# Moving half of four causal masks from VectorE to ScalarE and GpSimd, with two score banks instead of three

## The reference, cut to what matters

```
x = x + attention(layernorm(x))      # 16 heads of 16, chunks of 128 tokens
    q, k = elu(x Wq) + 1, elu(x Wk) + 1 ;  v = x Wv
    per chunk: scores = q k^T, kept where key <= query, else 0
               num = scores v + q S ;  S = S + k^T v
               out = num / (q . (running sum of k))
x = x + 0.5 * (silu(h w1 + b1) w2 + b2)   # h = layernorm(x) * gamma + beta
    w = (int - 128) * scale per group of 128 rows
```

## Time and profile before

| | |
|---|---|
| median of 3 runs | 1573.81 us (1571.97 to 1579.19) |
| the profiled execution's own time | 1571.97 us |
| its span | 1570.2 us |
| busy: PE, PEld, DVE, ACT, POOL | 97%, 84%, 83%, 72%, 43% |
| granted PE clock, mean | 0.993 |

### The profile page before, as it was taken

How to read it: one execution, slowest core, us unless ns; L and a number is a source line. 1 busy time by engine, 2 the same in 40 slices (tenths; PEclk the granted TensorE clock), 3 DMA queues, 4 the chain that set the end, 5 groups by cost and what they waited for, 6 DMA issues and landing times.

```text
span 1570.2 us, 40671 instructions
## 1 busy us (share of the span) xinstructions
PE 1529.8 (97%) x14820; PEld 1314.5 (84%) x14820; DVE 1307.1 (83%) x2587; ACT 1128.3 (72%) x1917; POOL 670.7 (43%) x466
## 2 busy tenths in 40 slices
PE   5799999999999999999999999999999999999997
PEld 4588888888888888888888888888888888888887
DVE  6888888888888888888888888888888888888875
ACT  4487677787777787777786776786776786777863
POOL 3244334544344444344444344443445443435443
PEclk9899999999999999999999999999999999999999
DMA  6945775445775556764556764447664556755450
GB/s 190 206 114 129 174 174 130 137 119 135 174 171 122 126 131 145 174 170 125 119 127 153 174 149 138 123 118 166 174 151 130 121 120 174 174 130 137 116 114 28
DMA packets 153945, 222.96 MB, mean 142 GB/s; under 512 B 20033, under 2 KB 71489, under 8 KB 153921
## 3 DMA queue, kind: packets, MB, share of 16 engines
q1 hardware_dynamic: 152560, 222.63, 58.8%
q10 hardware_dynamic: 1360, 0.01, 0.1%
HBM read 138.69 MB, written 83.89 MB: 142 GB/s over the span
## 4 chain that ended last, share of the span: by engine, by line
PE 84%; DVE 11%; issue 2%; DMA 1%; ACT 1%; SPq 1%; DVEq 0%; POOL 0%; ACTq 0%
PE ring L326 35%; PE num L494 7%; PE ring L388 6%; PE ring L389 6%; PE sc L326 5%; DVE probs L615 5%; PE sc L452 5%; PE num L461 3%; PE num L326 3%; PE state_acc L326 3%; DVE xt_lo L645 2%; PE ring L526 2%; PE state_acc L475 2%; DVE silu_f L701 2%; PE state_acc L452 1%
## 5 line engine op out<-in xcount | busy, mean ns | idle before, releaser
L1009 POOL TENSOR_TENSOR s_lo<-silu_f,s_hi 128x512 fp32r<-128x512 f32 x256 | 342.8, 1345 | 524.1 <-ACT s_hi L881 524.0
L615 DVE TENSOR_TENSOR probs<-sc,causal 128x512 f32<-128x512 f32 x416 | 270.6, 683 | 21.7 <-PE sc L452 18.6
L326 PE MATMUL ring<-w_hi,s_hi 128*128 128x256 f32 x992 | 281.5, 284 | 1.0 <-issue 1.0
L326 PE MATMUL ring<-w_lo,s_hi 128*128 128x256 f32 x992 | 278.3, 281 | 0.0
L326 PE MATMUL ring<-w_hi,s_lo 128*128 128x256 f32 x992 | 278.2, 280 | 0.0
L701 DVE SCALAR_TENSOR_TENSOR silu_f<-ring,scale,silu_f 128x512 f32<-128x512 f32 x222 | 166.3, 749 | 72.5 <-ACT silu_f L870 71.2
L326 PEld LDWEIGHTS ring<-w_hi,s_hi 128*128 128x128 f32 x992 | 186.8, 188 | 14.8 <-issue 13.5
L1025 POOL TENSOR_TENSOR qk<-qk,phi_q 128x512 f32<-128x512 f32 x64 | 83.1, 1298 | 264.6 <-DVE qk L668 264.6
L870 ACT ACTIVATE silu_f<-ring,bias,scale 128x512 f32<-128x512 f32 x217 | 168.4, 776 | 34.9 <-PE ring L389 33.9
L388 PE MATMUL ring<-gt_hi,w_q 128*128 128x512 f32 x441 | 192.5, 437 | 0.0
L326 PEld LDWEIGHTS ring<-w_lo,s_hi 128*128 128x128 f32 x992 | 187.0, 189 | 1.3
(11 more groups left out here) (189 smaller groups left out, 3859.2 us busy)
## 6 DMA issues: line engine op xcount, KB each, us to landing
k_stack<-k_rows SPq DMA_DIRECT2D x192, 256.0 KB, 4.0
q_stack<-q_rows SPq DMA_DIRECT2D x384, 128.0 KB, 6.1
k_rows<-silu_f SPq DMA_DIRECT2D x128, 256.0 KB, 3.7
q_rows<-probs SPq DMA_DIRECT2D x128, 256.0 KB, 4.0
x_in<-in_x SPq DMA_DIRECT2D x32, 512.0 KB, 8.3
xb<-in_x SPq DMA_DIRECT2D x32, 512.0 KB, 8.2
out<-clip SPq DMA_DIRECT2D x64, 256.0 KB, 7.8
silu_f<-in_q SPq DMA_DIRECT2D x2, 512.0 KB, 9.8
```

The lines of the kernel that those rows point to most:

```text
L326: last = e.matmul(target, a, b, start=(n == 0), stop=(n == 3 * len(pairs) - 1))
L615: masked[r].done(e.tensor_tensor(half_probs(u, r), score_bank(u, r)[:, :].rearrange("p (h q) -> p h q", h=HV), causal[:, None, :].to_broad ...
L1009: sl.done(e.tensor_tensor(s_lo[:, j, :], silu_f[:, j % SLOTS, :], s_hi[:, j, :].bitcast(F32), ALU.subtract))
```

## The change

It does six things.

1. The third bank for scores is given up: half r is always in `sc[r]`. A half now waits for the half r of the tile before it to be read.
2. For u = 2, 3, 4 and 5 the half r = 1 is no longer masked by DVE. ACT copies it out of PSUM into `probs` (`copy_scores`), and POOL multiplies it by `causal` in place.
3. DVE does `ffn_sum(2)` before `mask(1)`, and the second `snapshots` after `mask(3)` instead of `mask(2)`.
4. In step 0 `weights_2` moves on DVE from behind `mask(7)` to a place ahead of `mask(6)`, and `weights_2_lo` from the end of the step to the place that `weights_2` had. ACT's part moves with it. The products are made in place, in `res` and `x1`, and DVE no longer waits for `x_hat` to be free. POOL's wait for `bias_o` ahead of step 0 is dropped.
5. In step 31 PE does `fc2(1)` before the output product `wo`, not behind it, and DVE does `final(0)` before the adds of `wo`.
6. In step 32 DVE makes `res` ahead of `gt_lo`, and `ffn_scaled(1)` ahead of `ffn_sum(0)`.

```diff
-        SCORES = {(0, 0): 0, (0, 1): 1, (1, 0): 0, (1, 1): 1, (2, 0): 0, (2, 1): 1, (3, 0): 0, (3, 1): 2,
...
+        POOL_MASKS = (2, 3, 4, 5)
+        VE_MASKS = [range(U), [u for u in range(U) if u not in POOL_MASKS]]
+        masked = [ev(f"masked{r}", len(VE_MASKS[r])) for r in range(2)]
+        copied, po_masked = ev("copied", len(POOL_MASKS)), ev("po_masked", len(POOL_MASKS))
...
# pe_iteration, scores(u)
-                    before = score_before(u, r)
-                    if before:
-                        w.need(masked[before[1]], 0, before[0])
-                    elif score_bank(u, r) is state_acc:
-                        w.need(snap, 0)
+                    if r and u - 1 in POOL_MASKS:
+                        w.need(copied, 0, POOL_MASKS.index(u - 1))
+                    elif u:
+                        need_masked(w, u - 1, r)
...
-            if N:
-                fc2(1)
+            fc2(1)
             if A:
                 w.need(at_l)
                 for n in range(2):
                     pe_tokens(e, w, "o", (gt_hi, gt_lo), f"wo{n}", present, wo_pe)
-            if not N:
-                fc2(1)
...
# ve_iteration
-                for r in range(2):
+                for r in range(1 if u in POOL_MASKS else 2):
                     mask_half(e, w, u, r)
...
+            ffn_sum(2)
             if A:
                 mask(1)
-            ffn_sum(2)
-            if A:
                 snapshots(0)
...
                     if u == 5:
                         attention(0)
+                        if preparation[2]:
+                            preparation[2]()
...
-            if preparation[2]:
-                preparation[2]()
+            if preparation[1]:
+                preparation[1]()
             next_features(0)
...
# ac_iteration
+            def copy_scores(u):
+                if A and u in POOL_MASKS:
+                    w.need(sc_pe, 0, u)
+                    w.need(av_pe, 0, u - 2)
+                    copied.done(e.activation(half_probs(u, 1), sc[1][:, :].rearrange("p (h q) -> p h q", h=HV), ACT.Copy))
+
             for j in range(3, FT - 1):
                 ffn_scaled(j)
                 if j in (3, 5):
                     reciprocals_out((j - 3) // 2)
+                copy_scores(j - 1)
                 ffn_silu(j - 1)
...
# po_iteration
             for j in range(2, FT):
+                if A and j in POOL_MASKS:
+                    w.need(copied, 0, POOL_MASKS.index(j))
+                    po_masked.done(e.tensor_tensor(half_probs(j, 1), half_probs(j, 1),
+                                                   causal[:, None, :].to_broadcast([P, HV, P]), ALU.mult))
...
-            ve_iteration(e, -1, False, False, True, True, (projections, None, weights_1))
+            ve_iteration(e, -1, False, False, True, True, (projections, weights_1, None))
```

52 lines of the change are left out of this document (18 added, 34 removed).

## The result

The changed kernel takes 1585.32 us (median of 7 runs, 1584.51 to 1587.36), the kernel before, run beside it, 1571.97 us (median of 7, 1569.71 to 1579.19). The ratio is 1.0084, 95% interval 1.0065 to 1.0103: slower by 13 us. Its profiled execution took 1583.21 us with a span of 1581.5, against 1571.97 and 1570.2 before, so the traces have 11.3 us between them to explain.

What follows compares the result with a forecast made beforehand. The prediction took PE's long row of matmuls, with one hole per step, to bound the kernel. 1571.97 (span 1570.2) + 11.7 + 3.1 + 2.7 = 1589.5 us, taken as 1590; the range holding 8 in 10 was 1577 to 1604.

Steps and rivals of the forecast that it cites:

- The loop: In the 30 full steps, the projection comes 0.39 us later per step, 11.7 us in all.
- The step that failed: On ACT, four copies exceed its slack, so ffn_scaled(7) starts 0.6 us late, at about 762.9 instead of 762.26.
- the forecast's own rule: On DVE, ffn_sum(7) follows the start of ffn_scaled(7) after 0.78 us plus 0.12 for handing over, at 763.8.
- The rest of the chain: Late ffn_sum(7) delays tile 6's masks, second half of scores(7), values(6) to 766.20 and projection to 767.0, where it was 766.64.
- PE's hole: On PE ahead of the projection, a wait for DVE's xt_lo in which PE stands for 0.37 us each step.
- The hole's owner: Ahead of the projection, ACT's xt_hi also bounds xt_lo; only about 0.1 us of the 0.37 us is DVE's.
- Step 0: Early weights_2 waits for the scales, delaying the projection by 5.4 us; 2.3 won back at the end, sum +3.1 us.
- Steps 31 and 32: POOL's later queue and fc2(1) ahead of wo delay x_hat, gt_lo and ffn_sum(0); sum +2.7 us.
- Relief: In the loop, DVE's saved 2.4 us mask tile 6 sooner and close the hole; 1575 or 1561 us, chance 0.07.
- Only the ends: Copies fit into ACT's waits, the loop stays at 47.4 us and the ends cost 5.8; 1578 us, chance 0.13.
- POOL sets the pace: In the loop PE waits for POOL's products at four tiles, 1.2 us a step more; 1626 us, chance 0.12.

Runs made afterwards that it cites:

- experiment 11: The changed kernel with the weights late again in step 0 and steps 31 and 32 in the old order; 1579.57 us, ratio 1.0050.
- experiment 1: The changed kernel with the third score bank and its table put back; 1581.01 us, ratio 1.0058.
- experiment 5: The kernel before with only the second half of tile 5 copied by ACT and masked by POOL, three banks; 1578.83 us, ratio 1.0052.
- Experiment 6: The kernel before with PE's x_transposes moved ahead of values(5), no mask taken off DVE; 1572.87 us, ratio 1.0003.
- experiment 2: The kernel before with two score banks and nothing else changed; 1575.52 us, ratio 1.0023.
- experiment 3: The changed kernel with tile 5's second half masked by DVE again; 1592.62 us, ratio 1.0137.
- experiment 7: The kernel before with early x_transposes and tile 6's second half copied by ACT behind ffn_scaled(7) and masked by POOL; 1565.31 us, ratio 0.9959.
- Experiment 4: The kernel before with four more ACT copies per step into a spare tile nobody reads, DVE keeping all masks; 1580.18 us, ratio 1.0047.

## Why the prediction was right, and where it was off

The forecast, slower and about 1590 us, came true with 1585.3. It was made of three terms. The loop's was too large, three times by the means and twice like with like, and the two of the ends came out 1.8 us too small.

**The loop: +11.7 us forecast, +3.8 measured.** The step that failed is ACT's: `ffn_scaled(7)` was to start 0.64 us late. In the step shown, which has the long form as that of before, it starts 43.45 us behind the last projection instead of 42.99, so 0.46 late. The sum behind it was 2.0 + 0.4 - 1.8 = 0.6 between `ffn_scaled(3)` and `ffn_scaled(7)`; it measured 0.48. The four copies took 0.47 to 0.49 us each from start to start, as put in. But of the 0.4 us for waits on scores only some 0.1 came, ahead of the first copy, that of tile 2; the other three follow their neighbours at once.

From there the forecast's own rule holds: 762.26 + 0.46 + 0.76 + 0.12 = 763.60 for `ffn_sum(7)`, and it comes 44.33 us behind the last projection, which is 763.60 on the times of before. DVE had reached it at 763.45 before, so it is late by 0.15, where I had 0.35. The rest of the chain was right in its mechanism and its size: from 763.60 it gives 766.0 for `values(6)` and 766.8 for the projection, and measured are 766.03 and 766.85. `values(6)` is 0.59 late (forecast 0.76), PE's hole takes 0.38 of it, and the projection is 0.21 late, 0.20 over all long steps, where I had 0.39. A small excess that must first fill a hole is a difference of differences, and 0.18 us too much on ACT became 0.19 in every step. Thirty steps at 0.20 are 6.0 us. That the traces show 3.8 is the mix of forms, which my forecast knew nothing of, and which the change of the loop doesn't fix: with the same loop experiment 11 has 25 long steps. My own range for the step (0.15 to 0.7) holds the 0.20 and not the 0.13.

The forecast's two parts of the loss are both there, in other shares. 0.14 us come through ACT: `ffn_sum(7)` comes 44.32 us behind the last projection instead of 44.18, and it does so with three banks (experiment 1) and with the single copy ahead of `ffn_silu(5)` (experiment 5) as well. 0.06 come through the two banks: the projection follows `ffn_sum(7)` after 3.25 us instead of 3.19. I had blamed the sum of all four copies. How many there are matters little, since the copies of tiles 2 to 4 fall mostly into ACT's waits: between 90 and 1500 us ACT waited 33 us for the blocks of `fc1` before and waits 1 us now. What counts is the one next to `ffn_scaled(7)`.

**The hole's owner.** I wrote that it was ACT's `xt_hi` as much as DVE's `xt_lo`. Experiment 6 shows that `xt_hi` alone is not worth anything: 47.34 against 47.36. In the six traces with three banks and tile 6 left to DVE the projection comes 3.18 to 3.20 us behind `ffn_sum(7)`, which is that sum, two masks and two `xt_lo` on DVE; in the five of the changed loop it is 3.25, where PE's own row behind the second mask sets it; with two banks and tile 5 left to DVE (experiments 2 and 3) it is 3.48; only where a mask behind `ffn_sum(7)` was taken away and the transposes came early too is it 2.81. That the mask of tile 6 would do without the early transposes was not tried.

**Step 0: +3.1 forecast, +4.2 measured.** DVE waits for the scales (4.14 us; 3.8 forecast), and the projection of step 0 comes at 62.56 (60.7 forecast): the products start 1.0 us later than I had (56.76 against 55.8), and PE's row ahead of the projection, at the lower clock, lets it start only 1.05 us behind the end of `xt_lo`. (The term itself adds up to 5.4 + 0.1 - 2.3 = 3.2, not 3.1.) The time is partly won back behind it. In the changed kernel with the weights at the old place the projection of step 1 came at 106.4 and 104.3 us against 107.8, 107.8 and 107.6: 2.4 us on average. But the same code gave values 2.2 us apart. Over all traces the early place gave 105.5 to 107.8 us (five kernels' traces, mean 107.2) and the old place 103.6 to 107.1 (nine, mean 105.2), so about 2 of the 4.2 us are the edit's, and the other half can't be told from scatter.

**Steps 31 and 32: +2.7 forecast, +3.4 measured.** Counted from the last projection, the products of the FFN start 0.5 us later (1.1 forecast), `x_hat` 3.3 us (4.0), the first `gt_lo` 1.7 us (2.3) and `ffn_sum(0)` 3.4 us (2.7). So the chain to `gt_lo` was right in kind and too long, and behind it came 1.7 us where I had 0.4; the matmuls of `fc1` ran there at the lower clock, which was not in my sum. With the new order the tail took 96.5, 97.9 and 98.1 us, with the old one and the same loop 95.5 and 94.1. The difference of the means, 2.7 us, is the forecast's, which is in part luck: kernels with the old order and another loop gave 93.1 to 97.2 us.

**The rivals.** "Relief" did not come: DVE spent what it was relieved of on waiting for ACT. The Trainium skill, page "Perfetto Trace Analysis", section "Optimizing Scalar/DVE Operations", says that such a move may make sense when DVE is saturated (it was busy 83% here); experiments 5 and 7 show it failing with a mask that DVE does ahead of the wait and paying, together with the earlier transposes, with one behind it. "Only the ends" was nearer than its 0.13 says: the ends' part was 5.8 by its sum and 7.6 in the traces, and the loop's mean stayed within 0.13 us of the old step. "POOL sets the pace" is refuted: PE waited for POOL three times, 1.9 us in all.

**What stays open.** Why a step has the long or the short form isn't known, nor how many of each there are in the executions that were not traced; of the kernel before there is one trace. With 28 steps the form alone can be worth up to 3.9 us. Ratio and parts don't close for every kernel. Experiment 4 loses 7.8 us in the median with 3.7 in its trace's loop, and experiment 5 loses 7.1 with 3.9. In their traces the rest lies in the ends, where one trace differs from another of the same code by up to 2.2 us at the start and 1.6 in the tail, with the clock and the arrival of transfers. Single traces of the ends can't say how much of it the ACT copies of steps 0 and 31 cause.

## What to carry to other kernels

When work is moved to an engine with a low share, look for the instruction of that engine which the critical chain waits for, and place the added work behind it, not ahead: here one copy ahead of `ffn_scaled(7)` cost a step as much as four, and one behind it, together with earlier transposes, made the kernel faster. When work is taken off an engine, only what stands between its last wait and the hand-over to the bound engine counts; what stands ahead of that wait turns into waiting. And a forecast for a loop with one hole is a small difference: work out by how much the new lateness exceeds what the next engine was late anyway, then let the hole swallow its part, before multiplying by the number of steps. Before a difference of hundredths in a step is believed, look at the single steps: two forms of the same code, 0.14 us apart, can make or hide it in the mean.
